# An LSTM in a fused four-layer network: gate o gets a bank and an activation of its own, and VectorE's row loop is turned

## What is computed

```python
x = x + _L0_conv_ref(_ln_c(x), ...)          # involution
t = t + _L0_ffn_ref(_ln_t(t), ...)           # experts
x = x + _L1_conv_ref(_ln_c(x), ...)          # convolution
t = t + _L1_ffn_ref(_ln_t(t), ...)           # LSTM over 56 * 56 = 3136 tokens, 64 wide, 4 images

def step(carry, xs):                         # the LSTM
    h, c = carry
    i_t = sigmoid(xi_t + h @ V_i)
    g_t = tanh(xg_t + h @ V_c)
    o_t = sigmoid(xo_t + h @ V_o)
    c_new = h * c + i_t * g_t                # h stands where an LSTM has its forget gate
    h_new = o_t * tanh(c_new)
    return (h_new, c_new), h_new
```

## Time and profile before

| what | value |
|---|---|
| median of 3 runs | 4002.73 us (4000.49 to 4004.25) |
| the profiled execution | 4000.67 us, its span 3998.9 us |
| PE busy | 3586.2 us (90%) |
| DVE busy | 3382.6 us (85%) |
| ACT busy | 2526.5 us (63%) |
| POOL busy | 2159.1 us (54%) |

### The profile page before, as it was taken

How to read it: one execution, slowest core, us unless ns; L and a number is a source line. 1 busy time by engine, 2 the same in 40 slices (tenths; PEclk the granted TensorE clock), 3 DMA queues, 4 the chain that set the end, 5 groups by cost and what they waited for, 6 DMA issues and landing times.

```text
span 3998.9 us, 130353 instructions
## 1 busy us (share of the span) xinstructions
PE 3586.2 (90%) x35548; PEld 2658.7 (66%) x35548; DVE 3382.6 (85%) x21828; ACT 2526.5 (63%) x11666; POOL 2159.1 (54%) x3173
## 2 busy tenths in 40 slices
PE   6799999999898999999999999999989899988887
PEld 5666666666666666666666666666666666666665
DVE  6788888888888888888888888888888888887787
ACT  3366666666666666666666666666666666666565
POOL 6655565656565656555555555565655565652222
PEclk7955555555555555555555555555555555555555
DMA  5000000000000000000000000000000000000000
GB/s 74 2 1 1 1 1 1 1 1 1 1 1 1 1 1 1 1 1 1 1 1 1 1 1 1 1 1 1 1 1 1 1 1 1 1 2 1 1 1 1
DMA packets 44537, 11.06 MB, mean 3 GB/s; under 512 B 39913, under 2 KB 44010, under 8 KB 44490
## 3 DMA queue, kind: packets, MB, share of 16 engines
q1 hardware_dynamic: 42378, 10.05, 1.6%
q10 hardware_dynamic: 2112, 0.46, 0.1%
HBM read 7.29 MB, written 3.21 MB: 3 GB/s over the span
## 4 chain that ended last, share of the span: by engine, by line
PE 66%; DVE 14%; ACT 13%; issue 5%; POOL 1%; DVEq 0%; DMA 0%; ACTq 0%; POOLq 0%
PE GATES L1330 14%; PE YB L1150 10%; PE GATES L1400 9%; ACT O L736 7%; PE H1B L1144 7%; ACT G L732 6%; DVE O L975 6%; PE YB L1301 6%; PE TAPB L1137 6%; PE DB L1269 5%; DVE HR L979 5%; PE DB L1131 3%; PE H2B L1177 1%; PE H1B L1177 1%; PE H2B L1125 1%
## 5 line engine op out<-in xcount | busy, mean ns | idle before, releaser
L732 ACT ACTIVATE G<-GATES 128x12 f32<-128x12 f32 x3136 | 572.3, 182 | 1207.0 <-PE GATES L1400 1195.7
L1400 PEld LDWEIGHTS GATES<-HR,VW 128*128 128x128 f16 x6272 | 419.9, 106 | 605.7 <-issue 560.0
L968 DVE TENSOR_TENSOR_SCAN CT<-G,CT 128x12 f32<-128x12 f32 x3136 | 587.1, 187 | 268.0 <-ACT G L732 243.2
L1330 PE MATMUL GATES<-HR,VW 128*128 128x4 f16 x3136 | 532.2, 170 | 307.2 <-DVE HR L979 213.9
L736 ACT ACTIVATE O<-G 128x8 f32<-128x8 f32 x3136 | 662.1, 211 | 98.9 <-ACT G L732 0.2
L975 DVE RECIPROCAL O<-O 128x4 f32<-128x4 f32 x3136 | 567.5, 181 | 177.2 <-ACT O L736 0.2
L1396 PEld LDWEIGHTS <-VW 128*128 128x128 f16 x3136 | 457.4, 146 | 353.8 <-issue 317.2
L1400 PE MATMUL GATES<-H,VB 128*128 128x4 f16 x6272 | 616.8, 169 | 0.0
L987 DVE SCALAR_TENSOR_TENSOR CT<-HIST,CT 128x4 f32<-128x4 f32 x3136 | 521.4, 166 | 108.8
L1400 PE MATMUL GATES<-HR,VW 128*128 128x4 f16 x6272 | 613.1, 168 | 0.0
L1150 PE MATMUL YB<-HD,W 128*64 128x112 f32 x3840 | 595.5, 412 | 2.1 <-DVE HD L856 2.1
(11 more groups left out here) (242 smaller groups left out, 6995.0 us busy)
## 6 DMA issues: line engine op xcount, KB each, us to landing
out_dram<-OUT SPq DMA_DIRECT2D x112, 28.0 KB, 1.9
X<-in_x_dram SPq DMA_DIRECT2D x4, 672.0 KB, 11.3
STG<-in_L_ffn_w_dram SPq DMA_DIRECT2D x4, 512.0 KB, 12.5
U<-in_L_conv_U2s_dram SPq DMA_DIRECT2D x1, 972.0 KB
W<-in_L_ffn_w_dram SPq DMA_DIRECT2D x1, 512.0 KB, 11.7
X<-in_x_dram ACTq DMA_DIRECT2D x4, 112.0 KB, 3.0
S<-in_L_conv_S1s_dram SPq DMA_DIRECT2D x1, 108.0 KB
S<-in_L_conv_S2s_dram SPq DMA_DIRECT2D x1, 108.0 KB
```

The costliest lines, as they stand in the source:

```text
L732: act.activation(G6[:, :, 2:5], gates[c][:, w, :, :], ACT.Tanh, scale=1 / GSCALE).then_inc(step_in, 1)
L968: dve.tensor_tensor_scan(CELL.rearrange("z b k -> z (b k)"), G6[:, :, :].rearrange("z b k -> z (b k)")[:, 0::2], ADD3.rearrange("z b k -> ...
L1330: return pe.add_instruction(mybir.InstMatmult(name=nc.get_next_instruction_name(), engine=mybir.EngineType.PE, start_tensor_calc=False, st ...
L1400: last = pe.matmul(gates[c][:, w, :, SLOT[g]], wt[:, g].rearrange("z m c -> z (m c)"), digit, start=False, stop=True, skip_group_check=True)
```

## The change

Gate o leaves GATES. Its matmuls go into the first 224 columns of bank DB (`GATE_O`), and it becomes the last of each group of three. `gates_done` is raised by the second matmul of VB (gate i), `gate_o_done` by the third. ScalarE runs G's tanh on two gates, and a tanh of its own for o, whose output OT lies in the same PSUM bank DB. VectorE, behind its scan, turns OT into O5 with one scalar_tensor_tensor; the copy O on ScalarE is gone. The normalisation factors now go through H2B and the expert weights through H1B, with the waits that this needs: an expert's first product waits for the copy of the weights before it. A start flag would clear the whole bank, so ScalarE zeroes o's half (in t = 1 and 49), and the prefills of o, now the last three of nine, wait for `o1_done` of their own step. At the end of a row VectorE branches behind HIST, and h times c of t = 55 is done at the top of the next row. RED becomes a scalar_tensor_tensor of the same value.

```diff
-        PRE0={51: (0, 1, 2), 52: (3, 4), 53: (5, 6), 54: (7, 8)}, COPY=None, RSE=None)
+        PRE0={51: (0, 1), 52: (2, 3), 53: (4, 5), 54: (6, 7, 8)}, COPY=None, RSE=None)
...
-PRODUCTS = 3 + 2 * 3
-PRE1_AT = {3: (0, 1, 2, 3, 4), 6: (5, 6, 7, 8)}
-SLOT = (2, 0, 1)
+INPUTS = (("b", 0), ("b", 1), (0, 0), (0, 1), (1, 0), (1, 1), ("b", 2), (0, 2), (1, 2))
+PRODUCTS = len(INPUTS)
+FIRST_O = INPUTS.index(("b", 2))
+PRE1_AT = {3: (0, 1, 2, 3, 4, 5), 6: (6, 7, 8)}
+ZERO_AT = (1, 49)
+SLOT = (1, 0)
...
+        GATE_O = [DB[:, c * TOK:(c + 1) * TOK] for c in range(2)]
+        gate_o = [g.rearrange("z (b t) -> z t b", b=B) for g in GATE_O]
+        OT = DB[:, 448:448 + B]
...
         def spread(lstm):
-            return DB if lstm else GATES[1]
+            return H2B if lstm else GATES[1]
+
+        def weights_bank(lstm):
+
+            return H1B if lstm else DB
...
-                    act.activation(G6[:, :, 2:5], gates[c][:, w, :, :], ACT.Tanh, scale=1 / GSCALE).then_inc(step_in, 1)
+                    act.activation(G6[:, :, 2:5:2], gates[c][:, w, :, :], ACT.Tanh, scale=1 / GSCALE).then_inc(step_in, 1)
+                    act.wait_ge(gate_o_done, 1 + n + 1)
+                    act.activation(OT[:, :], gate_o[c][:, w, :], ACT.Tanh, scale=1 / GSCALE).then_inc(ot_done, 1)
                     act_registers(act, j, t, involution)
-
-                    act.wait_ge(step_in, 1 + 2 * n + 2)
-                    act.activation(O5[:, :, 1:5:3], G6[:, :, 3:4].broadcast_to([128, B, 2]), ACT.Copy, scale=O_MAX, bias=1.0)\
-                        .then_inc(o1_done, 1)
...
+                    for k in range(2):
+                        if t == ZERO_AT[k]:
+
+                            act.wait_ge(o1_done, 1 + n + 1)
+                            act.activation(GATE_O[1 - k], CST[:, CZERO:CZERO + 1].broadcast_to([128, TOK]), ACT.Copy).then_inc(oz_done, 1)
...
-                dve.tensor_tensor(RED[64:96, :], REDF, RED[64:96, :], ALU.subtract).then_inc(redlo_done, 1)
+                dve.scalar_tensor_tensor(out=RED[64:96, :], in0=REDF, scalar=1.0, in1=RED[64:96, :], op0=ALU.mult, op1=ALU.subtract)\
+                    .then_inc(redlo_done, 1)
...
+                    if t == 0:
+                        dve.wait_ge(h_done, before)
+                        h_times_c(dve, W - 1)
                     dve.wait_ge(step_in, first if t == 0 else 1 + 2 * n + 2)
...
+                    dve.wait_ge(ot_done, 1 + n + 1)
+                    dve.scalar_tensor_tensor(out=O5[:, :, 1:5:3], in0=OT[:, :].unsqueeze(2).broadcast_to([128, B, 2]), scalar=O_MAX,
+                                             in1=O5[:, :, 2:3].broadcast_to([128, B, 2]), op0=ALU.mult, op1=ALU.subtract)\
+                        .then_inc(o1_done, 1)
                     fill_registers(dve, j, t, involution, lstm, experts)
...
-                    dve.wait_ge(h_done, 1 + n + 1)
-                    dve.scalar_tensor_tensor(out=ADD3[:, :, 2], in0=HIST[:, t, :], scalar=0.5, in1=CELL[:, :, 2],
-                                             op0=ALU.mult, op1=ALU.mult).then_inc(step_in, 1)
+                    if t < W - 1:
+                        dve.wait_ge(h_done, 1 + n + 1)
+                        h_times_c(dve, t)
...
+                    if k == FIRST_O:
+                        pe.wait_ge(o1_done, 1 + (j - LAG) * W + t + 1)
+                    last = prefill(pe, 1, k, lstm)
...
-                pe.wait_ge(si_done, 1 + NG * j + k)
+                if lstm:
+                    pe.wait_ge(dbs_done, 1 + NG * j + k)
+                else:
+                    pe.wait_ge(si_done, 1 + NG * j + k)
...
+                    if k == FIRST_O and lstm:
+                        pe.wait_ge(o1_done, 1 + (j - LAG) * W + t + 1)
+                    last = prefill(pe, 0, k, lstm)
...
-                        for g in range(1, 3):
-                            last = pe.matmul(gates[c][:, w, :, SLOT[g]], wt[:, g].rearrange("z m c -> z (m c)"), digit,
-                                             start=False, stop=True, skip_group_check=True)
-                    last.then_inc(gates_done, 1)
+                        last = pe.matmul(gates[c][:, w, :, SLOT[1]], wt[:, 1].rearrange("z m c -> z (m c)"), digit,
+                                         start=False, stop=True, skip_group_check=True)
+                        if wt is VB:
+                            last.then_inc(gates_done, 1)
+                        if wt is VW and t - 1 in ZERO_AT:
+                            pe.wait_ge(oz_done, 1 + 2 * (j - LAG) + ZERO_AT.index(t - 1) + 1)
+                        last = pe.matmul(gate_o[c][:, w, :], wt[:, 2].rearrange("z m c -> z (m c)"), digit,
+                                         start=False, stop=True, skip_group_check=True)
+                    last.then_inc(gate_o_done, 1)
```

More of the change, by code:

```diff
@@ L225, in build_program @@
         TC5 = CT[:, 32:52].rearrange("z (b k) -> z b k", k=5)
-        gates = [g[:, 0:HALF * B * 3].rearrange("z (k b t) -> z t b k", b=B, k=3) for g in GATES]
+        gates = [g[:, 0:HALF * B * 2].rearrange("z (k b t) -> z t b k", b=B, k=2) for g in GATES]
+        GATE_O = [DB[:, c * TOK:(c + 1) * TOK] for c in range(2)]
+        gate_o = [g.rearrange("z (b t) -> z t b", b=B) for g in GATE_O]
+        OT = DB[:, 448:448 + B]
         REDF = TAPB[64:96, TOK:2 * TOK]
@@ L278, in build_program @@
             "conv_done slot3_done slot2_done res4a_done res4_done")
[L281 removed]
+        (dupx_done, x4_done, pre0_done, pre1_done, gates_done, gate_o_done, oz_done, step_in, ot_done, o1_done, cell_done,
          t_done, rec_done, hd1_done, hd2_done, h_done, ocopy_done, oadd_done, ostored) = lstm_sems = sems(
[L283 removed]
+            "dupx_done x4_done pre0_done pre1_done gates_done gate_o_done oz_done step_in ot_done o1_done cell_done "
             "t_done rec_done hd1_done hd2_done h_done ocopy_done oadd_done ostored")
@@ L336, in _ @@
             for n, c in enumerate(counted):
-                sp.sem_inc(c, 16 if c is ostored else 2 if c is step_in else 1 + left_out.get(c, 0))
+                sp.sem_inc(c, 16 if c is ostored else 1 + left_out.get(c, 0))
                 if n == len(counted) // 2:
@@ L691, in act_fill @@
                 act.wait_ge(hd_done, 1 + NG * j + k)
-                act.activation(DBS[:, :], DB[:, 0:EG * 2 * TOK], ACT.Copy).then_inc(dbs_done, 1)
+                act.activation(DBS[:, :], weights_bank(lstm)[:, 0:EG * 2 * TOK], ACT.Copy).then_inc(dbs_done, 1)
         def act_registers(act, j, t, involution):
@@ L960, in fill_registers, with h_times_c, dve_row @@
                     dve.lower_ap(window(j, k, 2 * h, 2))
-        def dve_row(dve, j, first, involution, lstm, experts, pre):
+        def h_times_c(dve, t):
+            dve.scalar_tensor_tensor(out=ADD3[:, :, 2], in0=HIST[:, t, :], scalar=0.5, in1=CELL[:, :, 2],
+                                     op0=ALU.mult, op1=ALU.mult).then_inc(step_in, 1)
+        def dve_row(dve, j, first, before, involution, lstm, experts, pre):
             for t in range(W):
@@ L973, in dve_row @@
                         dve.reg_add(first, first, 2 * W)
+                        dve.reg_add(before, before, W)
                     dve.wait_ge(o1_done, 1 + n + 1)
@@ L1105, in _, with prefill @@
             dve.reg_mov(first, 1 + 2)
+            before = dve.alloc_register("before")
+            dve.reg_mov(before, 1)
             with rows(dve, LAG, H) as j:
-                dve_row(dve, j, first, True, True, True, True)
+                dve_row(dve, j, first, before, True, True, True, True)
             with rows(dve, H, H + LAG) as j:
-                dve_row(dve, j, first, False, True, True, True)
-        def prefill(pe, c, k):
-            if k < 3:
-                return pe.matmul(GATES[c][:, SLOT[k] * TOK:(SLOT[k] + 1) * TOK], BX[:, k].rearrange("z m c -> z (m c)"),
-                                 ONEH[:, :], start=(k == 0), stop=False, skip_group_check=True)
-            d, g = divmod(k - 3, 3)
+                dve_row(dve, j, first, before, False, True, True, True)
+        def prefill(pe, c, k, lstm):
+            d, g = INPUTS[k]
+            bank = GATE_O[c] if g == 2 else GATES[c][:, SLOT[g] * TOK:(SLOT[g] + 1) * TOK]
+            if d == "b":
+                return pe.matmul(bank, BX[:, g].rearrange("z m c -> z (m c)"), ONEH[:, :],
+                                 start=(k == 0 or (k == FIRST_O and not lstm)), stop=False, skip_group_check=True)
             xs = X4S[:, :].rearrange("z (p q w) -> z p q w", p=2, q=Q)[:, :, :, c * HALF:(c + 1) * HALF]
-            return pe.matmul(GATES[c][:, SLOT[g] * TOK:(SLOT[g] + 1) * TOK].rearrange("z (q p t) -> z p q t", q=Q, p=2),
+            return pe.matmul(bank.rearrange("z (q p t) -> z p q t", q=Q, p=2),
                              UX[:, d, g].rearrange("z m c -> z (m c)"), xs, start=False, stop=False, skip_group_check=True)
@@ L1238, in pe_fill @@
                         pe.wait_ge(step_in, 1 + 2 * (j - LAG) * W)
```

(16 more changed lines are left out.)

14 lines of the change are left out of this document (6 added, 8 removed).

## The result

| | before | after |
|---|---|---|
| time, median of 4 runs each | 4002.98 us | 4108.43 us |
| range of the runs | 4000.49 to 4004.25 | 4106.86 to 4109.38 |
| span of the profiled execution | 3998.9 | 4105.1 |

The changed kernel takes 1.0261 times as long (95% interval 1.0248 to 1.0275). The sign of the forecast was right. The size was not: +15 us were predicted and +105 came (+106 between the two profiled spans), and 4108 lies above the range.

A forecast was written before the change was run, and what follows sets the result against it. The LSTM's serial dependences were taken to bound nearly every step; -69 us from ordinary steps and costs of 42, 7, 8, 2, 6, 14 and 5 summed to +15 us, a forecast median of 4018 us, range 3967 to 4062.

The forecast's parts named there:

- ordinary step: Each of the 3136 serial LSTM steps falls from 1.207 to 1.185 us, a gain of 69 us.
- TensorE waits for o, t = 6 and 54: Prefills waiting for o1_done hold up TensorE's queue: 0.47 us in t=6, 0.28 in t=54, together 42 us.
- steps with DB and conv: Six steps a row with dispatch-weight and conv matmuls need 1.73 us against the recurrence's 1.71: cost 7 us.
- row boundary, t = 1: Moved h times c and later reciprocal cost 8 us at the row boundary; fp32 means in t=1 may add 2.
- registers: In 250 steps a second fused register instruction between scan and reciprocal costs 0.02 to 0.03 us each: 6 us, bounds 0 and 25.
- held O5, RED: New VectorE instruction held after L814 and L861 until the scan ends: 14 us; RED as scalar_tensor_tensor: 5 us.
- the o path: G, scan, new instruction, reciprocal, H5, VB: 1.18 to 1.19 us, about 0.01 longer than via c's tanh; sets the step.
- Rival B: In ordinary steps the new instruction is slower, scan to reciprocal above 0.31: step 1.21, about +66, 4068 us; chance 0.14.
- C: Rival: TensorE's wait for o doesn't bite since o1_done comes much earlier than 0.89: 3976 us; chance 0.18, shared with a variant.
- D: Rival: G's tanh starts no earlier because ScalarE is still in a fill: about +80 us; chance 0.03.
- A: Rival: ordinary step 1.175, set by c's chain; 100 us won but 97 lost in single steps, 4000 us; chance 0.20.
- The c path: Ordinary step's chain from VB through G's tanh, scan, tanh of c, HR and H5 back to VB: 1.17 to 1.18 us.

The follow-up runs named there:

- the kernel of 509 instructions: Kernel after with VectorE's row loop cut from 522 to 509 instructions (registers of two steps computed together, two waits moved): 4066.94 us, 1.016 of before.
- the kernel without the o path: Kernel with 511 VectorE instructions, late o prefills, memsets and tensor_tensor at t=8, with O5 made from a constant ahead of the scan: 4469.26 us in one execution.
- the kernels with late o prefills: First of them: the 509-instruction kernel with gate o's three prefills and their wait put last in TensorE's fills of t=6 and t=54: 4024.02 us, 1.0052 of before.
- the memset: Late-prefill kernel plus a one-element VectorE write at SBUF partition 0 behind RED and behind DP's low part: 4013.73 us, 1.0029 of before.

## Why the prediction was wrong, point by point

The sum of +15 against what the traces give (us; the change of a step's excess over an ordinary one, times the rows that have it; the loading of code is the difference of steps 0, 27 and 28 to the kernel of 509 instructions or an ordinary step):

| term | predicted | found |
|---|---|---|
| ordinary step | -69 | -23 |
| TensorE waits for o, t = 6 and 54 | +42 | +48 |
| steps with DB and conv | +7 | -2 |
| row boundary, t = 1 | +10 | +2 |
| registers | +6 | +6 |
| held O5, RED | +19 | +15 |
| loading of code | not there | +59 |
| sum | +15 | +105 |

**The missing term.** The prediction asked of each added instruction how long it takes and what it waits for, and never how many there are: 465 and 56 are 521. So this term stood at nothing in the sum. It is 59 us by the medians of the steps and about 61 by the kernel with the shorter loop, and it is shown from both sides, by padding the kernel before and by shortening the kernel after. None of the rivals had it. It alone doesn't account for the miss: without it the change would still cost 46 us and not 15, mainly because of the next term.

**The ordinary step, the mis-sized term.** The mechanism was right: the o path sets the step, at G to scan 0.21, O5 0.09 behind the scan, H5 when the reciprocal is done. The step came out as 1.185; the same links measured at t = 34, with the predicted value in parentheses: G to scan 0.213 (0.21), scan to reciprocal 0.288 (0.285), reciprocal to H5 0.217 (0.215), H5 to VB 0.249 (0.24), VB to G 0.233 (0.23). They add to 1.200, and the predicted ones to 1.18 (the forecast took 1.185). Four links were rounded down by 0.002 to 0.003 each. The fifth is a real error: H5 to VB is 0.249, not 0.24, as H5 lasts 196 ns in this kernel and 187 in an ordinary step of before. The 0.20 of H5 in the earlier trace rows, where it starts behind a wait, had shown it. Over 3136 steps 0.015 are 47 us. So the gain was 23 us and not 69. Predicting a serial loop of this length to 0.2% needs the step to 2 or 3 ns, and the rows shown give 10.

Rival B, named with its deciding point above 0.31, fell: 0.288. C fell: the wait bit. D fell. A was not reached. The c path was sized rightly at 1.17 to 1.18; the kernel without the o path shows 1.178.

**The waits of TensorE** were right in place and near in size: 0.55 against 0.47 in t = 6 and 0.31 against 0.28 in t = 54. In t = 6 the prefill starts 0.98 behind the first matmul, not 0.89, because o's tanh starts 0.21 behind G there and not 0.07 (ScalarE in t = 6 of the kernel after):

```profile
2019.13 0.40 ACT L665 ACTIVATE TAPB<-TAPB,BN 32x112 f32<-32x112 f32 x1
2019.70 0.18 ACT L744 ACTIVATE G<-GATES 128x8 f32<-128x8 f32 x1 [0.18 <-PE GATES L1445]
2019.91 0.16 ACT L746 ACTIVATE DB<-DB 128x4 f32<-128x4 f32 x1
```

L665 writes PSUM at partition 64, and o's tanh is the next to write PSUM at 0. It looks like the hold seen on VectorE, but it wasn't tried alone. Its price is left in the kernels with late o prefills, as steps 6 and 7 of 1.236 and 1.26: 0.09 us a row, 5 us.

**The held O5** was right: 0.22 behind the scan, 0.13 over steps 12 and 13 and, with what the place of RED adds, 0.16 over 8 and 9. The Trainium skill's rule (VectorE: DVE Perf Modes, section Two Vector instructions with no wait between them) holds here in the case where only the output's place differs, and the memset moved the hold as it says. **RED's other form** was costed at 5 us and is free. **Registers**: 6, as forecast, but as 0.02 in each of t = 17, 18, 32, 37, 42 and 47. **The boundary** was costed at +8 and the turning alone saves about 4; the step that failed is the 0.50 from HIST to h times c, which took over a figure from a loop in which the branch stands last. **The zeroing activations** cost nothing that shows: steps 2 and 50, whose o matmul waits for them, are 1.200 and 1.199.

**DB and conv**: these steps are 1.200 like the others. The forecast gave them 1.205; with an ordinary step of 1.200 a limit of their own doesn't show.

## What to carry to other kernels

Count the instructions of each engine's loop body before and after an edit; an added instruction of 0.16 us can still push the loop over what the engine holds, and then each pass pays one to three microseconds (here 1.2, 1.4 and 2.9). In the profile it shows as idle time "issue" behind a branch together with packets in the instruction queue. And where an instruction must wait for another engine, put it last in its queue's stretch: the wait itself was not shortened here, only what stood behind it, and that was worth 43 us.
